# One gate burst per batch, silu in two bursts of two blocks, and one residual sum moved to TensorE, in a Mamba block with a linear layer

## The reference

```
xi  = ctx @ in_proj.T                          # (b, 512 channels, 512 steps)
u   = silu(causal 4-tap conv(xi) + conv_b)
dt_low, B, C = split(u @ x_proj.T)             # 16, 16, 16
dt  = softplus(dt_low @ dt_proj.T + dt_b);  A = -exp(A_log)
state[n] = state[n] * exp(dt * A[n]) + dt * u * B[n]     # along the steps
y   = (sum over n of C[n] * state[n] + D * u) * silu(layernorm(x))
x1  = x + y.T
out = x1 + layernorm(x1) @ (sum of 8 factors) / sqrt(8) + bias
```

## Time and profile before

| | us |
|---|---|
| median of 3 runs | 481.11 (479.55 to 481.75) |
| the profiled execution's own time | 481.48 |
| its span, first to last instruction | 479.7 |
| VectorE busy | 451.2 (94% of the span) |
| TensorE busy | 438.1 (91%) |
| GpSimd busy | 429.4 (90%) |
| ScalarE busy | 363.0 (76%) |
| mean granted TensorE clock | 0.979 of full |

### The profile page before, as it was taken

The page is one execution under the profiler, slowest core; times in us unless marked ns, Lnnn a source line. Parts: engine busy times, 40 slices in busy tenths (PEclk is TensorE's granted clock), DMA queues, the critical chain, the costliest instruction groups (busy, mean ns, idle before and its releaser), DMA issues.

```text
span 479.7 us, 4156 instructions
## 1 busy us (share of the span) xinstructions
PE 438.1 (91%) x1119; PEld 187.4 (39%) x1132; DVE 451.2 (94%) x324; ACT 363.0 (76%) x595; POOL 429.4 (90%) x226
## 2 busy tenths in 40 slices
PE   8998798899999779899989798899989998989996
PEld 5242342434433243433434243343434443334432
DVE  5798899999999999999999997999998999999996
ACT  4678795887689798796899879697899876654422
POOL 4369999899999999997999979798999969999982
PEclk9999899999999969999999889999999999999999
DMA  5799746339992000100793000000495000000002
GB/s 193 260 350 359 198 81 142 51 78 217 292 362 77 1 0 0 53 15 0 239 412 122 0 23 0 1 23 0 118 396 237 1 22 23 22 22 22 2 0 88
DMA packets 16848, 53.97 MB, mean 113 GB/s; under 512 B 1828, under 2 KB 2084, under 8 KB 15800
## 3 DMA queue, kind: packets, MB, share of 16 engines
q1 hardware_dynamic: 15384, 45.14, 26.3%
q0 software_dynamic: 1152, 8.39, 8.7%
q10 hardware_dynamic: 288, 0.18, 0.1%
HBM read 49.24 MB, written 4.46 MB: 112 GB/s over the span
## 4 chain that ended last, share of the span: by engine, by line
POOL 39%; DVE 18%; issue 18%; PE 15%; DMA 5%; ACT 3%; SPq 2%; POOLq 0%; DVEq 0%
POOL h L1103 30%; DVE dA L956 12%; POOL h L1096 6%; PE y L528 6%; DMA b_rep<-bc_scratch 4%; DVE h L956 3%; DVE h L962 2%; PE work L406 2%; POOL dtu L1089 2%; PE work L516 1%; SPq L339 1%; ACT dA L786 1%; PE dA L432 1%; PE y L618 1%; SPq L334 1%
## 5 line engine op out<-in xcount | busy, mean ns | idle before, releaser
L1103 POOL TENSOR_TENSOR h<-b_rep,dtu 128x1024 f32<-128x1024 f32 x127 | 303.7, 2440 | 12.3 <-DMA b_rep<-bc_scratch 11.5
L528 PE MATMUL y<-h,ident 128*128 128x512 f32 x508 | 242.4, 615 | 30.9 <-DVE h L962 28.1
L956 DVE TENSOR_TENSOR_SCAN dA<-dA,h 128x1024 f32<-128x1024 f32 x94 | 214.9, 2287 | 13.8 <-ACT dA L786 13.3
L786 ACT ACTIVATE dA<-dt,a_neg 128x512 f32<-128x512 f32 x256 | 165.6, 680 | 76.2 <-DVE h L962 62.2
L528 PEld LDWEIGHTS y<-h,ident 128*128 128x128 f32 x508 | 94.6, 194 | 165.1 <-issue 107.2
L962 DVE TENSOR_TENSOR h<-dA,c_rep 128x1024 f32<-128x1024 f32 x93 | 113.4, 1219 | 2.1
L1096 POOL TENSOR_TENSOR h<-h,c_rep 128x1024 f32<-128x1024 f32 x34 | 81.4, 2394 | 13.5 <-DVE h L956 13.4
L956 DVE TENSOR_TENSOR_SCAN h<-dA,h 128x1024 f32<-128x1024 f32 x34 | 77.5, 2278 | 0.1
L516 PE MATMUL work<-fsum,xnT 128*128 128x512 f32 x64 | 28.8, 592 | 0.0
L406 PE MATMUL work<-ctx_sb,w_in 128*128 128x512 f32 x60 | 28.1, 598 | 0.3 <-DMA ctx_sb<-ctxT 0.3
L930 DVE SCALAR_TENSOR_TENSOR acc<-work,chan,acc 128x511 f32<-128x511 f32 (+2 forms) x30 | 21.6, 730 | 1.3 <-ACT acc L665 1.2
(11 more groups left out here) (130 smaller groups left out, 397.4 us busy)
## 6 DMA issues: line engine op xcount, KB each, us to landing
b_rep<-bc_scratch SPq DMA_DIRECT2D x32, 512.0 KB, 9.6
c_rep<-bc_scratch SPq DMA_DIRECT2D x32, 512.0 KB, 9.7
fsum<-factors POOLq DMA_DIRECT2D x8, 1024.0 KB, 8.1
x<-x SPq DMA_DIRECT2D x4, 1024.0 KB, 7.6
out<-x SPq DMA_DIRECT2D x16, 256.0 KB, 2.0
ctx_sb<-ctxT SPq DMA_DIRECT2D x3, 512.0 KB, 5.5
ctx_sb<-ctxT SPq DMA_DIRECT2D x2, 256.0 KB, 4.4
w_in<-w_inT SPq DMA_DIRECT2D x1, 384.0 KB, 5.2
```

The costliest lines, as they stand in the source:

```text
L528: mm = pe.matmul(y[:], ident[:], h[:, (s * PAIRS + j) % H_RING, i, :], start=False, stop=(j == sum_order(s)[-1] and i == 1))
L786: act.activation(dA[:, j % 2, i, :], dt[:, k % 2, :], ACT.Exp, scale=a_neg[:, k, 2 * j + i:2 * j + i + 1]).then_inc(exp_done, 1)
L956: dve.tensor_tensor_scan(pair if on_pool(s * PAIRS + j) else decay, decay, pair, 0.0, ALU.mult, ALU.add).then_inc(scanned, 1)
L1103: pool.tensor_tensor(h[:, (s * PAIRS + j) % H_RING], b_rep[:, j], dtu[:, k % 2, :].unsqueeze(1).to_broadcast([P, 2, L]), ALU.mult).then_in ...
```

## The change

- GATE_SLOTS becomes (7, 2, 2, 4) and `gate_half` becomes `gate_batch`: all four gates of a batch in one burst, behind pair 7 of step 0, pair 2 of steps 4 and 8, pair 4 of step 12. The waits for `gated` stand before the first and the fourth block.
- The silu of the next batch's convolution: two blocks behind pair 5 of a batch's second step, two behind pair 4 of its third.
- POOL_C of steps 4 and 8 becomes (0, 4) in place of (0, 2): GpSimd makes the product of the fifth pair there, VectorE that of the third. The count on each engine stays; the sum order becomes (1, 0, 2, 3, 5, 4, 6, 7).
- Softplus of step 12 stands behind pair 2 instead of pair 0. The statistics of steps 4 and 8 stand behind pair 5 instead of 3 (step 12 has none).
- Step 4 joins TENSOR_RESIDUAL: `add_x1(4)` goes from VectorE, one identity matmul goes to TensorE, `x1_evac(4)` to ScalarE, behind pair 3 of step 5.

```diff
-POOL_C = ((0, 4), (0,), (0, 2), (0, 2), (0, 2), (0, 2), (0, 2), (0, 2, 4), (0, 2), (0, 2, 4), (0, 2), (0, 2, 4), (0, 2),
+POOL_C = ((0, 4), (0,), (0, 2), (0, 2), (0, 4), (0, 2), (0, 2), (0, 2, 4), (0, 4), (0, 2, 4), (0, 2), (0, 2, 4), (0, 2),
           (0, 2), (0, 2), (0, 2))
-SOFTPLUS_SLOTS = (2, 2, 2, 2, 0, 2, 2, 2, 0, 2, 2, 2, 0, 2, 2, 2)
-GATE_SLOTS = ((4, 6), (2, 5), (2, 5), (2, 5))
+SOFTPLUS_SLOTS = (2, 2, 2, 2, 0, 2, 2, 2, 0, 2, 2, 2, 2, 2, 2, 2)
+GATE_SLOTS = (7, 2, 2, 4)
+SILU_SLOTS = {1: 5, 2: 4}
-STATS_SLOTS = (5, 3, 5, 3, 3, 3, 3, 3, 3, 3, 3, 3, 3, 3, 3, 3)
-TENSOR_RESIDUAL = (0, 1, 2, 6, 8)
+STATS_SLOTS = (5, 3, 5, 3, 5, 3, 3, 3, 5, 3, 3, 3, 5, 3, 3, 3)
+TENSOR_RESIDUAL = (0, 1, 2, 4, 6, 8)
...
-            def gate_half(b, half):
+            def gate_batch(b):
                 act.wait_ge(g_nb, (b + 1) * KB)
-                if b > 0:
-                    act.wait_ge(gated, b * KB - 1 + half)
-                for k in range(half * (KB // 2), (half + 1) * (KB // 2)):
+                for k in range(KB):
+                    if b > 0 and k in (0, KB - 1):
+                        act.wait_ge(gated, b * KB - (1 if k == 0 else 0))
                     act.activation(gate[:, k, :], x1_block(b, k), ACT.Silu, bias=g_r[:, 2, k:k + 1],
                                    scale=g_r[:, 1, k:k + 1]).then_inc(g_done, 1)
...
-                    if k == 0 and j in GATE_SLOTS[b]:
+                    if k == 0 and j == GATE_SLOTS[b]:
                         act.preload_act_table_set("silu_and_others")
-                        gate_half(b, GATE_SLOTS[b].index(j))
+                        gate_batch(b)
                         act.preload_act_table_set("natural_log_exp_and_others")
-                    if j == 4 and k in (1, KB - 2) and b + 1 < BATCH:
+                    if j == SILU_SLOTS.get(k) and b + 1 < BATCH:
                         act.preload_act_table_set("silu_and_others")
-                        silu_blocks(b + 1, *((0, KB - 1) if k == 1 else (KB - 1, KB)))
+                        silu_blocks(b + 1, (k - 1) * (KB // 2), k * (KB // 2))
                         act.preload_act_table_set("natural_log_exp_and_others")
```

## The result

The changed kernel takes 476.38 us (median of 5, 474.72 to 477.73), the kernel before 481.11 (479.55 to 483.71): ratio 0.9897, 95% interval 0.9867 to 0.9927. In a second session it took 474.49 against 481.92: 0.9868 (0.9820 to 0.9917). Forecast was 475.0, between the two.

A forecast was written before the change was run, and what follows sets the result against it. VectorE's own work plus 13.3 us idle for ScalarE's decays was taken to set the end. Step terms summed to 6.1 us: 481.48 to 475.4, taken as 475.0 since that execution was 0.4 above the median; range 472.5 to 478.5.

The forecast's parts named there:

- Bursts: ScalarE's gates: 5.56 us per batch instead of 8.26, four times; only the table load itself is paid.
- Step 0: Gate burst behind pair 7: scan 1.0 at 55.4 instead of 57.51, 2.1 us gained, 1.4 idle left.
- Steps 4 and 8: Gate burst behind the third pair, covered by 1.26 more: 0.4 us gained in step 4, 1.0 in step 8.
- Step 9: Silu behind pair 5: 2.2 and 0.2 idle instead of 3.16, the 0.5 before 9.3 gone; 1.3 us gained.
- Step 5: add_x1(4) off VectorE (0.44) and silu moved (0.65 idle instead of 0.95): 0.75 us gained together.
- Step 12: Softplus behind pair 2, one gate burst behind pair 4: 1.32 + 0.99 - 1.55 = 0.75 us gained.
- Gone in 8, undecided in 4: TensorE's half-clock stretches: assumed gone in step 8, undecided in step 4; -1.5 and +4 us kept for the range.
- No stretch at half clock between steps 4 and 9: Sign that would show the forecast: TensorE never at half clock between steps 4 and 9.
- rival 1: TensorE's clock falls in steps 5, 9 and 12 or 13: 3.1 us gained, 478.0; chance 0.17.
- Rivals 3 and 4: Whole kernel: ScalarE's lead spent, 4.8 slower, 486, chance 0.04; stalls only change place, 480, chance 0.08.
- rival 2: TensorE never falls, waits at 9.3, 9.5 and step 7's end go, stalls overlap: 2 us more, 473.0; chance 0.13.
- Rival 4: Whole kernel: stalls only change place, at the forecast's price plus a half: 4 us more, 480; chance 0.08.

The follow-up runs named there:

- e1: Changed kernel with two more table loads in the middle of each of the four gate bursts; 487.03 us, ratio to before 1.0102.
- e2: Changed kernel with POOL_C of steps 4 and 8 back at (0, 2), the third pair's product on GpSimd; 477.52 us, ratio to before 0.9909.
- e8: Kernel before with only step 4 put into TENSOR_RESIDUAL; 482.28 us, ratio to before 0.9994.
- e10: Kernel before, unchanged, profiled a second time; 480.33 us, one run.
- e7: Changed kernel, unchanged, run and profiled again; 474.49 us, its profiled execution 479.23.
- e5: Changed kernel with step 4's x added by VectorE again, TensorE still doing the matmul of x as idle work; 475.49 us, ratio to before 0.9871.
- e4: Changed kernel with step 4 taken out of TENSOR_RESIDUAL, so VectorE adds x; 477.04 us, ratio to before 0.9899.
- e11: Changed kernel with SCALE_SLOTS (1, 4, 6, 7), step 9's silu burst behind slot 6's conv tap, step 5's x matmul done twice; 473.33 us, ratio to before 0.9817.
- e12: Second profile of e4's kernel: changed kernel with step 4's x added by VectorE; 475.85 us, one run.

## Why the prediction was right

**The bound and the method.** VectorE's own work plus its waits for the decays: e1 shows that a microsecond on ScalarE in front of an exhausted lead is a microsecond of the kernel, and the nine stretches came out within 0.35 of the forecast each. Positions in ScalarE's order, pass lengths and the beat give each wait; only in step 9 was part of the agreement luck (below).

**Bursts.** 5.54 for 5.56. The next task starts 1.29 after a load's start, so nothing but the load is paid. The Trainium skill (ScalarE: Activation LUTs, "What ACT_TABLE_LOAD costs") adds a drain of about 1380 ns to each switch; the measurement does not bear it out here. The eight loads saved returned 10.1 us of ScalarE with the rest of the change, as the rows had it, not 21.

**Step 0.** 1.30 left before 1.0. C of pair 7 was there. What I had not said: scan 1.1 follows GpSimd's input by 0.1 us (start 59.22, input ready 59.12), so in this profile a shorter burst would gain next to nothing. From 1.0 to 1.1 it takes 2.37 here and 2.21 in e1, and step 1 is 27.07 us long here and 26.88 to 26.91 in the other profiles with the silu in its new place.

**Steps 4 and 8.** 0.47 and 1.23 for 0.4 and 1.0; e2 confirms the cover by 1.26. GpSimd's lost lead cost nothing: VectorE never waits for it in steps 4 to 9.

**Step 9.** 1.33 for 1.3, but the old price came from the first profile of before, and 0.9 of it was chance (e8, e10). Against the other two profiles the step gains only 0.4: 2.90 before 9.5 became 0.34 and 2.04 before 9.5 and 9.6. The term's agreement with the first profile is luck in this part. With the second profile of before the steps gained 5.75 in place of 6.6; taken over all four profiles of the two kernels, the gain from scan 0.3 to 15.7 lies between 4.4 (e10 against e7) and 6.6. The medians differ by 4.7 in the first session and 7.4 in the second, and do not say more closely what the change is worth.

**Step 5.** 0.82 for 0.75. Both halves hold: the silu's move gives 0.36 (28.76 to the 28.40 of e5; 0.30 forecast) and VectorE's work 0.46 (0.44 forecast). The clock has no part in these 0.82, since its fall cost nothing in the old order; it decides whether they are kept (e4, e7). That was not in the term.

**Step 12.** 1.08 for 0.75: the one term that was clearly too small. The decays of 12.5 ended 1.34 late instead of 1.55, which is 0.2 of the 0.33; the other 0.1 is not accounted for.

**The clock.** "Gone in 8, undecided in 4": no profile with the new gates has a stretch at half clock between 265 and 280 us, all three with the old ones have. Of the waits that the prediction names for the stretch at 165.8 us, only the one of 1.92 stands before it; that of 3.10 lies inside. "No stretch at half clock between steps 4 and 9" did not come true: the changed kernel's first profile has one at 186.9 us and e7 two (170.6 and about 191 us); only the one at 170.6 cost more than 0.1 us. In step 5 rival 1 happens in part: e7's execution paid 1.4 (2 forecast), and that execution, 479.23 against a median of 474.49, also had the latest start of all (scan 0.3 at 40.99). The prediction read in the Trainium skill (TensorE: Matmul & The Clock Gate, "HAM oscillation — how this bites in real kernels") that fewer, longer bursts on ScalarE are the worse pattern for TensorE. That fits e11, where one longer wait at the end of step 9 came before a fall of the clock, and not the change as a whole, which raised the mean clock from 0.979 to 0.992 in the first profiles.

Rivals 3 and 4 did not happen: ScalarE entered the bursts of 4.2 and 8.2 with leads of 2.7 and 3.1. Nor did rival 2: the waits before 9.5 and 9.6 stayed (0.34 and 2.04). Two figures of the prediction do not come out of its own numbers. Rival 4's "4 more" on 475.0 is 479, not 480. The clock's "-1.5 and +4" is not what the range uses, -2.5 and +3.5; the first median, 476.38, lies inside either.

## What to carry to other kernels

When one engine is busy 94% and the rest of its time is waits for another's side tasks, price a move by place, not by the helper's busy share: lead at entry plus the interval of the bounding engine, less the burst and what stands behind it. Put the longest burst behind the longest interval, and move work between engines so that the long interval is there; the same edit can gain or lose by what stands in front of it (e8). A wait of TensorE without work can be worth filling, even with a product that is thrown away, where something in a fixed order waits for its next result: here the clock fell in one profile of nine with the wait partly filled and in five of five without. And a single profile of before is not enough to price a wait that hangs on TensorE's clock (step 9).

## What the runs showed of the hardware

Steps without a change of TensorE's clock mostly repeat within 0.02 us from execution to execution and kernel to kernel; of the scatter that the profiles show, up to 4 us lie in the first 40 us and up to 1.7 in whether, when and how long the clock is at half. Stretches at half clock inside the steps were between 3.4 and 10.3 us long. In the same wait of 3.73 us one of 6.8 and one of 3.4 began (e4, e12), at prices of 1.7 and 0.2.

A table load costs ScalarE 1.28 to 1.30 us and nothing besides: the next pass starts 1.29 after it (49.98 to 51.27), and eight more loads made the kernel 10.56 us longer from scan 0.3 to 15.7 (e1).
